# A recurrent block with a mixture of experts: the gathered token blocks are transposed through DRAM pieces and VectorE's 32x32 squares instead of TensorE

## What is computed

```python
xn = _layernorm(x, axis=-1)
x = x + _L0_attn_ref(xn, ...) + _L0_ffn_ref(xn, w_router, w_fc, w_proj)

def _L0_attn_ref(x, ...):          # gated linear recurrence, then a dense gate/up/down layer
    h = _rmsnorm(x, pre_norm_w)
    a = sigmoid(h @ w_a + decay_bias); i_gate = sigmoid(h @ w_i); v = h @ w_v
    rec_out = _chunked_scan(a, sqrt(clip(1.0 - a * a, 1e-08)) * (i_gate * v))
    x = x + rec_out @ out_proj_w
    h2 = _rmsnorm(x, ffn_norm_w)
    gate, up = split(h2 @ w_gate_up, 2, axis=-1)
    return x + silu(gate) * up @ w_down

def _L0_ffn_ref(x, w_router, w_fc, w_proj):   # 8 experts, the best 2 of each token
    top_vals, top_idx = top_k(x_flat @ w_router, 2)
    probs = softmax(top_vals, axis=-1)
    h = square(relu(einsum('nc,ecd->ned', x_flat, w_fc)))
    y = einsum('ned,edc->nec', h, w_proj)
    return einsum('nec,ne->nc', y, w_tok)
```

## Time and profile before

| | before |
|---|---|
| median of the runs | 288.89 us |
| span of the profiled execution, first to last instruction | 286.9 us |
| TensorE busy | 279.4 us (97%) |
| VectorE busy | 202.7 us (71%) |
| ScalarE busy | 170.9 us (60%) |
| GpSimd busy | 145.8 us (51%) |
| granted TensorE clock | full in all 40 slices |

### The profile page before, as it was taken

One profiled execution on the slowest core, in us unless ns is written; L12 is line 12 of the kernel. 1 busy time (PEld: TensorE's weight loads), 2 busy tenths in 40 slices (PEclk: granted clock), 3 DMA queues, 4 the chain that ended last, 5 costly groups with the idle time before them and its releaser, 6 DMA issues.

```text
span 286.9 us, 5651 instructions
## 1 busy us (share of the span) xinstructions
PE 279.4 (97%) x1825; PEld 249.2 (87%) x1825; DVE 202.7 (71%) x467; ACT 170.9 (60%) x365; POOL 145.8 (51%) x138
## 2 busy tenths in 40 slices
PE   6999999999999999999999899999999999999995
PEld 5888988888988898898998789989989999888895
DVE  3899899989988978836558686555446545446973
ACT  3797967999759555536675545437477545432331
POOL 5498020433750135864877777666786776620000
PEclk9999999999999999999999999999999999999999
DMA  6999990017995011444244444344344534449922
GB/s 210 344 377 383 386 409 0 0 11 113 243 267 115 0 40 39 76 68 64 56 77 70 75 64 73 62 69 61 61 78 77 84 62 56 55 84 358 331 75 73
DMA packets 32584, 36.92 MB, mean 129 GB/s; under 512 B 4390, under 2 KB 29740, under 8 KB 32524
## 3 DMA queue, kind: packets, MB, share of 16 engines
q0 software_dynamic: 9616, 13.01, 28.2%
q1 hardware_dynamic: 20672, 21.31, 22.4%
q10 hardware_dynamic: 2268, 2.23, 2.2%
HBM read 24.68 MB, written 13.96 MB: 135 GB/s over the span
## 4 chain that ended last, share of the span: by engine, by line
PE 90%; DVE 5%; POOL 2%; issue 2%; ACT 1%; POOLq 0%; ACTq 0%; DVEq 0%
PE ps L396 75%; PE ps L656 6%; PE ps L479 5%; PE ps L400 1%; PE ps L492 1%; PE ps L413 1%; DVE hT_lo L1087 1%; POOL rn L1504 1%; DVE Wpj_lo L1247 1%; DVE stats L1059 0%; DVE X L1080 0%; DVE dec L1118 0%; POOL Waiv_raw L1541 0%; PE ps L507 0%; DVE xgT_lo L1322 0%
## 5 line engine op out<-in xcount | busy, mean ns | idle before, releaser
L1552 POOL DMA_INDIRECT xg<-xh_dram,gather_u x39 | 46.6, 1195 | 47.4 <-DVE picks L1314 34.8
L1561 POOL DMA_INDIRECT acc_dram<-yb,gather_u x39 | 61.9, 1587 | 16.3 <-issue 9.4
L396 PE MATMUL ps<-h2T_lo,Wgu_hi 128*128 128x512 f32 (+1 forms) x132 | 42.9, 386 | 0.0
L396 PE MATMUL ps<-h2T_hi,Wgu_hi 128*128 128x512 f32 (+1 forms) x132 | 40.9, 391 | 0.0
L396 PE MATMUL ps<-h2T_hi,Wgu_lo 128*128 128x512 f32 (+1 forms) x132 | 40.1, 385 | 0.0
L396 PE MATMUL ps<-Wd_hi,guT_hi 128*128 128x256 f32 x128 | 36.3, 284 | 0.1
L1331 DVE TENSOR_TENSOR aT_lo<-ps,aT_hi 128x256 fp32r<-128x256 f32 x39 | 16.6, 425 | 27.9 <-ACT aT_hi L911 21.1
L396 PE MATMUL ps<-Wd_hi,guT_lo 128*128 128x256 f32 x128 | 36.1, 282 | 0.0
L396 PE MATMUL ps<-Wd_lo,guT_hi 128*128 128x256 f32 x128 | 36.1, 282 | 0.0
L1252 DVE TENSOR_TENSOR gu<-gu,ps 128x512 f32<-128x512 f32 x31 | 21.2, 684 | 14.0 <-PE ps L396 10.9
L869 ACT ACTIVATE gu<-ps 128x512 f32<-128x512 f32 x31 | 18.4, 595 | 20.2 <-PE ps L396 20.2
(11 more groups left out here) (190 smaller groups left out, 683.7 us busy)
## 6 DMA issues: line engine op xcount, KB each, us to landing
sums<-acc_dram SPq DMA_DIRECT2D x8, 512.0 KB, 7.8
acc_dram<-zero SPq DMA_DIRECT2D x1, 2176.0 KB, 14.8
Wgu_raw<-in_L_attn_w_gate_up_dram SPq DMA_DIRECT2D x4, 512.0 KB, 9.3
Wfc_raw<-in_L_ffn_w_fc_dram SPq DMA_DIRECT2D x4, 512.0 KB, 13.7
xh_dram<-X ACTq DMA_DIRECT2D x4, 512.0 KB, 7.9
Wpj_raw<-in_L_ffn_w_proj_dram SPq DMA_DIRECT2D x4, 512.0 KB, 9.8
X<-in_L_attn_x_dram SPq DMA_DIRECT2D x3, 512.0 KB, 6.3
out_dram<-X SPq DMA_DIRECT2D x3, 512.0 KB, 4.8
```

Of the source, the lines that this page charges most:

```text
L396: return nc.tensor.matmul(dst, lhs, rhs, start=start, stop=stop, skip_group_check=group)
L1552: pool.indirect_dma_start(out=xg[i % XG][:, :], out_offset=None, in_=xh_dram, in_offset=bass.IndirectOffsetOnAxis(ap=gather_u[:, i:i + 1], ...
L1561: pool.indirect_dma_start(out=acc_dram[i % 2], in_=yb[i % YB][:, :], in_offset=None, compute_op=ALU.add, out_offset=bass.IndirectOffsetOnA ...
```

## The change

A gathered block no longer goes from `xg` to TensorE. SP stores its 256 columns to a DRAM tensor `xs_dram` in pieces of 32 columns (128 rows x 8 pieces of 128 bytes) and loads them back so that each partition receives two runs of 512 bytes: partition 32 q + r then holds, of column group q of each half, the rows 4 r to 4 r + 3. One VectorE instruction, `V.transpose`, turns eight 32x32 squares and writes `xgT_raw`, the transposed block, over the bytes that `xgT_lo` takes later. `block_in` on ACT and DVE read `xgT_raw` in SBUF in place of PSUM bank 2. TensorE's 78 transposes of `xg` are gone, T2 stays. `block_turn(i + 1)` stands on DVE right behind `block_weight(i)`. The wait on `t1_done` in `gather` becomes one on `xs_stored`, that in `block_weight` one on `xg_loaded`. PE's wait of the first block for `gu_ready` moves to the first T2. The region of the small tiles grows by 384 bytes.

```diff
+    XQ = 2
+    Q = 32
...
+    xs_dram = nc.dram_tensor("xs_dram", [NB, D // Q, P, Q], F32, kind="Internal").ap()
+    xs_in = xs_dram.rearrange("n m s c -> n s m c")
+    xs_out = xs_dram.rearrange("n (k q) (i g) c -> n (q i) k (g c)", k=K, g=P // Q)
...
@@ SP @@
+            def store_block(i):
+                sp.wait_ge(xg_loaded[i % XG], 16 * (i // XG + 1))
+                sp.dma_start(xs_in[i], xg[i % XG][:, 0:D].rearrange("p (m c) -> p m c", c=Q)).then_inc(xs_stored[i % XG], 16)
+
+            def load_quarters(i):
+
+                sp.wait_ge(xs_stored[i % XG], 16 * (i // XG + 1))
+                if i >= XQ:
+                    sp.wait_ge(turned, i - XQ + 1)
+                sp.dma_start(xq[i % XQ][:, :, :, :].rearrange("p k g c -> p k (g c)"),
+                             xs_out[i]).then_inc(xq_loaded[i % XQ], 16)
+
+            for i in range(NB):
+                store_block(i)
+                if i:
+                    load_quarters(i - 1)
+            load_quarters(NB - 1)
...
@@ PE, expert_in @@
-                if i < NB:
-                    pe.wait_ge(xg_loaded[i % XG], 16 * (i // XG + 1))
-                    if i:
-                        pe.wait_ge(xg_split, i)
-                    else:
-                        pe.wait_ge(gu_ready, FIRST - 1)
-                    block_transpose(T1, xg[i % XG], t1_done)
...
@@ ACT, block_in @@
-                act.wait_ge(t1_done, i + 1)
+                act.wait_ge(turned, i + 1)
                 if i >= 2:
                     act.wait_ge(fc_done, i - 1)
-                A.activation(xgT[i % 2][0][:, :, :].rearrange(flat), ps[:, T1, 0:D], ACT.Copy).then_inc(xg_hi, 1)
+                A.activation(xgT[i % 2][0][:, :, :].rearrange(flat), xgT_raw[i % 2][:, :, :].rearrange(flat),
+                             ACT.Copy).then_inc(xg_hi, 1)
...
@@ DVE @@
-                dve.wait_ge(t1_done, i + 1)
+                dve.wait_ge(xg_loaded[i % XG], 16 * (i // XG + 1))
...
+            def block_turn(i):
+
+                if i < NB:
+                    dve.wait_ge(xq_loaded[i % XQ], 16 * (i // XQ + 1))
+                    if i >= 2:
+                        dve.wait_ge(fc_done, i - 1)
+                    V.transpose(xgT_raw[i % 2][:, :, :].rearrange("p k (r g) -> p k g r", g=P // Q),
+                                xq[i % XQ][:, :, :, :]).then_inc(turned, 1)
...
             weights_lo(14)
+            block_turn(0)
...
                         block_weight(i)
+                        block_turn(i + 1)
...
@@ POOL, gather @@
-                    pool.wait_ge(t1_done, i - XG + 1)
+                    pool.wait_ge(xs_stored[i % XG], 16 * (i // XG))
                     pool.wait_ge(p_ready, i - XG + 1)
```

More of the change, by code:

```diff
@@ L156, in recurrent_moe_block @@
                 put(f"guT{u}_lo", [P, S], F32R, guT_at + 4 * KB * u + 2 * KB)) for u in range(2)]
-        moe_at = room(20 * KB - 256)
+        moe_at = room(20 * KB + 128)
         at_lane = put("at_lane", [P, TOP * T, P], F16, moe_at)
@@ L186, in recurrent_moe_block @@
         hi_f, lo_f = small("hi_f", [P, TOP * T]), small("lo_f", [P, TOP * T])
-        assert over[0] <= moe_at + 20 * KB - 256
+        assert over[0] <= moe_at + 20 * KB + 128
         over = [Wpj_lo_at + 12 * KB]
@@ L194, in recurrent_moe_block @@
         xg = [small(f"xg{u}", [P, ROW]) for u in range(XG)]
-        xgT = [(small(f"xgT{u}_hi", [P, K, P], F32R), small(f"xgT{u}_lo", [P, K, P], F32R)) for u in range(2)]
+        xgT, xgT_raw = [], []
+        for u in range(2):
+            hi = small(f"xgT{u}_hi", [P, K, P], F32R)
+            xgT_raw.append(put(f"xgT{u}_raw", [P, K, P], F32, over[0]))
+            xgT.append((hi, small(f"xgT{u}_lo", [P, K, P], F32R)))
         act_e = [small(f"act_e{u}", [P, D]) for u in range(2)]
@@ L198, in recurrent_moe_block @@
         yb = [small(f"yb{u}", [P, D]) for u in range(YB)]
-        assert over[0] <= moe_at + 20 * KB - 256
+        xq = [small(f"xq{u}", [P, K, P // Q, Q]) for u in range(XQ)]
+        assert over[0] <= moe_at + 20 * KB + 128
         h2 = [h2_first] + [put("h2", [P, J, D], F32, cum_at)] * (B - 1)
@@ L238, in recurrent_moe_block @@
         xg_loaded = [sem(f"xg_loaded{u}") for u in range(XG)]
-        t1_done, xg_hi, xg_split = sem("t1_done"), sem("xg_hi"), sem("xg_split")
+        xs_stored = [sem(f"xs_stored{u}") for u in range(XG)]
+        xq_loaded = [sem(f"xq_loaded{u}") for u in range(XQ)]
+        turned, xg_hi, xg_split = sem("turned"), sem("xg_hi"), sem("xg_split")
         fc_done, relu_done, act_ready = sem("fc_done"), sem("relu_done"), sem("act_ready")
@@ L272, in recurrent_moe_block @@
         TX, LOGIT = 0, 7
-        T1, T2, FC, PJ = 2, 3, 6, 7
+        T2, FC, PJ = 3, 6, 7
         DOWN = 4
@@ L690, in expert_out @@
                         pe.wait_ge(a_split, i - 1)
+                    else:
+                        pe.wait_ge(gu_ready, FIRST - 1)
                     block_transpose(T2, act_e[(i - 1) % 2], t2_done)
@@ L1318, in _ @@
             flat = "p k n -> p (k n)"
+            def block_turn(i):
[5 more added lines that the diff above has]
+                                xq[i % XQ][:, :, :, :]).then_inc(turned, 1)
             def block_in(i):
                 dve.wait_ge(xg_hi, i + 1)
-                V.tensor_tensor(xgT[i % 2][1][:, :, :].rearrange(flat), ps[:, T1, 0:D],
+                V.tensor_tensor(xgT[i % 2][1][:, :, :].rearrange(flat), xgT_raw[i % 2][:, :, :].rearrange(flat),
                                 xgT[i % 2][0][:, :, :].rearrange(flat).bitcast(F32), ALU.subtract).then_inc(xg_split, 1)
```

## The result

The changed kernel takes **300.6 us** (median of four runs, 297.96 to 301.65) against 288.85 beside it: a ratio of 1.040, 95% interval 1.037 to 1.043, 11.75 us slower. The forecast was 291.4 and its range ended at 300.5. The profiled execution was the longest of the four, with a span of 299.9 us.

The account below looks back on a forecast made before the run. TensorE, busy 97% of the span, was taken to bound the kernel. +0.8 and +1.7 made +2.5 on the span of 286.9, and with 2.0 between span and median 291.4 us; range 288.3 to 300.5.

Parts of the forecast that it names:

- The trip's term, +1.7: Store and load through DRAM before the turn: 7.8 us from weight to turn, late at six blocks, +1.7 us in all.
- I take 3.4: Gather's time to landing within the trip: 3.4 us, between 3.0 and at most 4.6.
- I take 3.0: Landing time of a block's load on SP's queue: 3.0 us, between bounds of 2.2 and 4.3.
- The first four blocks lay ready: At the start, POOL's 14.27 us idle ahead of the fifth gather was to cover the first four blocks' trips.
- I take 0.34: The transposing instruction's cost on VectorE: 0.34 us, between 0.21 and 0.61.
- The floor from FC to FC: Shortest step through square, weight, turn and `xgT_hi` to the next block's FC: 3.28 us.
- The base of +0.8: Transposes saved on TensorE against the turn in VectorE's chain, over all blocks: +0.7 to +0.8 us net, without late trips.
- Rival 2: A dear turn on VectorE: at 0.61 us, 17 places cost 0.27 more each, +4.6, so 296 us; chance 0.12.
- rival 3: A cheap turn on VectorE, 0.21 us, and a hidden trip under 7.2 us: 287.5 us; chance 0.10.
- 19 steps 0.22 less, 3 with 0.13: TensorE's saving: 19 steps on its own pace give 0.22 us each, -4.2; 3 others 0.13 each, -0.4.
- There is room, though not without queueing: Crowding of the DMA queues: 2.8 of 3.77 us a step used with the new transfers, against 1.7 of 3.9 before.
- Rival 1: The trip sets every step's pace, (trip + 3.2) / 3; at 9.0 us, +11 us, so 300 us; chance 0.24.

Follow-up runs that it names:

- the turn alone: The changed kernel without store and load, VectorE's turn reading the gathered block directly, rows and columns in another order: 292.67 us, 1.014.
- the own order: The changed kernel with SP issuing store i, load i in place of store i+1, load i: 294.49 us, 1.020.
- the version with turn and weight early: The changed kernel with SP issuing store i, load i, and block i+1's turn and weight moved ahead of `block_middle(i - 1)` on VectorE: 290.18 us, 1.005.

## Why the prediction was right or wrong

The side was right, and each of its two mechanisms was found: saved matmuls eaten by a chain through VectorE, and a trip that comes late. Both terms were too small, and a third, the clock, was missing; the sum said +2.5 and the runs +11.75.

- **The trip's term, +1.7, was mis-sized; it measured 7.6** (11.75 less the 4.1 of the turn alone). The parts were right at the median: 0.92 to the gather, 3.1 for it, 0.46 for the store's issue, 3.1 for the load, together 7.6 against a forecast 7.8. The step that failed is "I take 3.4" and "I take 3.0", one number for all 39 blocks. The landings spread: gathers from 2.8 to 4.9, loads from 2.1 to 4.5, and a gather behind GpSimd's own work starts 0.6 later. The eight trips whose turn waited took 8.2 to 10.4 us from weight to turn. A trip that is early earns nothing, one that is late is paid nearly whole: VectorE waited 8.4 us in 8 places, and the steps of those eight blocks are together 8.1 us longer than in the turn alone.
- **The clock was priced at nothing.** The forecast reads a full clock and has no term for a clock that falls. In the profile it was at half for 3.4 us behind the stand at block 28; the step into block 29 took 4.53 us, where the turn alone has 3.56, though its turn waited for no load. That puts some 1.0 us of the profiled run down to the clock. Of the four runs only the shortest, 297.96 us, has a mean granted clock of 1.000; the others, 300.27 to 301.65, have a mean of 0.989 to 0.994. So the 7.6 hold a share of the clock, whose size in the median no run shows.
- **Which blocks.** Foretold late: 13, 15, 28, 29, 31, 38. Late in the trace: 3, 13, 14, 15, 23, 28, 32, 36. The short steps were rightly named as the weak places, but 23 and 36 stand behind regular ones.
- "The first four blocks lay ready" failed for block 3: its load stood behind the store of block 4, whose gather began only after the first weight; it landed 4.9 us later, and block 3's step grew from 4.13 to 6.29.
- **The turn, "I take 0.34", was mis-sized.** It measures 0.48 on VectorE's chain and 0.67 to its reader. The floor from FC to FC came out at 3.53 instead of 3.28, in the turn alone ahead of block 28: 1.77 + 0.08 + 0.67 + 1.01. The base of +0.8 measured +4.1 (the turn alone). Rival 2 had the price (0.61) and gave 296; the turn's 0.64 is also past the 0.55 that was named as a sign of it. What was held against it, that no plain 256-column instruction takes over 0.43, is true of `TENSOR_TENSOR` only: `SCALAR_TENSOR_TENSOR` on X takes 0.475.
- The argument in rival 3, that the turn writes every fourth element and so won't be cheap, was the right one and was used too little. Written straight, the turn costs +1.8 where the forecast's base was +0.8.
- The saving of regular steps: "19 steps 0.22 less, 3 with 0.13" was 4.6, and the turn alone shows 3.2. Every other regular step has only 0.1 to give (3.98 to 3.88).
- Recurrence steps: 8 x 0.34 forecast, 8 x 0.48 measured. T blocks and third blocks: +1.5 forecast, +2.8. The blocks behind T: +0.4 forecast, -0.2. Blocks 0 and 1: +0.7 forecast, +1.1.
- "There is room, though not without queueing": right. The DMA share of 0.78 costs nothing by itself.
- The Trainium skill, DMA: Bandwidth & Descriptors, Anatomy of one DMA, from which the estimate of 2.3 us was worked out, gives its fit for transfers issued by GpSimd; these are issued by SP. In the own order, where the store has landed before its load is issued, the load lands in 2.3 us at the median, which agrees all the same; in the changed order it takes 3.1, and the spread decided, of which that estimate says nothing.
- **Rival 1** has the time (300) by luck and not the way: it let all steps run at (trip + 3.2) / 3. In the trace regular steps read 3.78 to 3.88, as the forecast had it, and single blocks carry the loss.

## What to carry to other kernels

A wait whose slack is only a few tenths must be reckoned with the spread of what it waits for, not with its median: early arrivals earn nothing and late ones add up. Before work is put on another engine, look at where in that engine's order it stands: with the transposes gone in both, the same turn cost 4.1 us behind the weight and brought 3.3 us in a pause three instructions earlier. In an in-order DMA queue look at what each issue stands behind, and free the buffers that start a chain as early as their last reader can be moved; here one 0.16 us instruction, moved up by a step, was worth 7.9 us. And a stall can cost more than its length: behind one of 3.6 us TensorE ran at half its clock for 3.4 us.

## What was not expected of the hardware

- Writing turned squares with a stride of four f32 elements takes 641 ns instead of 441 for 128x256. The Trainium skill, SBUF — State Buffer, the note on "cachelines" in Door 1: The DMA port swizzle, has lines of 16 bytes and a penalty for each access that goes to a new one. A stride of four f32 is such an access each time, and the runs agree in direction. The same note calls 4 fp32 the distance that one can stride for free; read as a stride of four, the measurement is against it. That the mechanism is this one, no run here shows.
- 39 stores in pieces of 128 B and 39 loads in pieces of 512 B raised the DMA share from 0.43 to 0.78 with no measurable effect on the time (1.0003); what GpSimd waited for scatters was 4.6 us before and 3.7 with them.
- A load issued right behind a store on the same queue landed 0.8 us later (3.1 us at the median in the changed kernel against 2.3 in its own order).
- The clock fell to half behind a stand of TensorE of 3.58 us in the changed kernel and one of 2.15 us in the version with turn and weight early, for about 3.5 us each time; behind one of 2.18 us it stayed full. What decides between them is not shown.
- The changed kernel's four runs lie 3.7 us apart, those of the turn alone 0.3. Landings that scatter and the clock that follows both come in; the run with the full clock is the shortest by 2.3 us.
